# Norms behind message passing computed inside its last step, and front rows and columns stored in four parts

## What is computed

```
xn  = layernorm(x)
h_t = xn;  three times: h_t = GRU_t(segment_sum((h_t @ W_t)[src] * (type == t), dst), h_t)
g   = leaky(layernorm(xn + h_0 + h_1 + h_2) * gamma + beta)      # slope 0.1
x1  = x + g + attention(xn)
out = x1 + experts(layernorm(x1))                                 # top 2 of 8 experts
```

## Time and profile before

| | us |
|---|---|
| median of 3 runs (3695.35, 3696.33, 3705.32) | 3696.33 |
| the profiled execution, its own time | 3672.03 |
| its span, first to last instruction | 3670.3 |
| TensorE busy in it | 2890.1 (79%) |
| VectorE busy | 1716.4 (47%) |
| ScalarE busy | 804.0 (22%) |
| GpSimd busy | 1475.2 (40%) |

### The profile page before, as it was taken

The page is one execution under the profiler, slowest core; times in us unless marked ns, Lnnn a source line. Parts: engine busy times, 40 slices in busy tenths (PEclk is TensorE's granted clock), DMA queues, the critical chain, the costliest instruction groups (busy, mean ns, idle before and its releaser), DMA issues. The chain is left out here.

```text
span 3670.3 us, 50411 instructions
## 1 busy us (share of the span) xinstructions
PE 2890.1 (79%) x15593; PEld 1858.2 (51%) x15593; DVE 1716.4 (47%) x3495; ACT 804.0 (22%) x1522; POOL 1475.2 (40%) x1508
## 2 busy tenths in 40 slices
PE   1589688889488888977888889688888933899991
PEld 1344455555264444555444446454444533788881
DVE  4379677771155555534454554254555556100002
ACT  1321244442211111141111113111111111233320
POOL 0000144440466666326666660666666200111124
PEclk6689798885699999988999999799999965799995
DMA  1200000001444444333444442433333133022213
GB/s 42 79 1 1 1 0 0 0 2 31 151 126 135 120 131 129 115 112 114 134 129 131 135 132 71 144 113 116 114 116 115 46 80 116 24 83 82 81 47 95
DMA packets 172350, 311.49 MB, mean 85 GB/s; under 512 B 26928, under 2 KB 125199, under 8 KB 171922
## 3 DMA queue, kind: packets, MB, share of 16 engines
q0 software_dynamic: 62016, 168.51, 16.0%
q1 hardware_dynamic: 110162, 140.82, 11.9%
HBM read 241.74 MB, written 67.49 MB: 84 GB/s over the span
## 5 line engine op out<-in xcount | busy, mean ns | idle before, releaser
L1420 POOL DMA_INDIRECT g_ring<-h_rows,idx x780 | 771.7, 989 | 369.6 <-issue 207.1
L1148 PE MATMUL g_pagg<-g_onehot,g_ring 128*128 128x144 f16 x4704 | 430.1, 231 | 229.5 <-issue 227.4
L1148 PEld LDWEIGHTS g_pagg<-g_onehot,g_ring 128*128 128x128 f16 x4704 | 342.1, 100 | 499.8 <-issue 483.0
L1319 DVE TENSOR_TENSOR g_agg<-g_agg,g_pagg 128x288 f32 x585 | 264.6, 452 | 574.9 <-remote 332.8
L1420 POOL DMA_INDIRECT g_ring<-xn_rows,idx x390 | 383.4, 983 | 188.3 <-issue 102.5
L864 POOL TENSOR_TENSOR mq_Fl<-mq_F,mq_Fh 128x448 f16<-128x448 f32 x168 | 191.4, 1166 | 490.4 <-ACT mq_Fh L849 483.0
L1322 DVE SCALAR_TENSOR_TENSOR g_onehot<-iota_keys,shift,keys 128x288 f16<-128x288 f16 x585 | 298.7, 512 | 0.9 <-issue 0.6
L1225 PE MATMUL g_pr<-g_agg,g_wc 128*128 128x448 f32 (+1 forms) x576 | 234.3, 526 | 23.0 <-DVE g_agg L1319 12.9
L1268 ACT ACTIVATE g_nT<-g_t,g_bi 128x448 f32<-128x448 f32 (+1 forms) x144 | 89.5, 622 | 704.2 <-DVE g_t L1361 499.2
L1225 PE MATMUL g_pi<-g_agg,g_wc 128*128 128x448 f32 (+1 forms) x576 | 228.8, 517 | 7.0 <-issue 6.6
L1939 DVE TENSOR_TENSOR f_ys<-f_bank,f_b 128x256 f32<-128x256 f32 x58 | 24.6, 424 | 444.1 <-PE f_bank L1888 430.2
(11 more groups left out here) (337 smaller groups left out, 4211.5 us busy)
## 6 DMA issues: line engine op xcount, KB each, us to landing
f_w<-in_L_ffn_W SPq DMA_DIRECT2D x16, 1024.0 KB
h_cols<-g_hn SPq DMA_DIRECT2D x36, 448.0 KB
h_rows<-g_rows SPq DMA_DIRECT2D x36, 448.0 KB
g_hT<-h_cols SPq DMA_DIRECT2D x36, 448.0 KB
g_ring<-h_rows,idx POOLq DMA_INDIRECT x780
g_hT<-xn_cols SPq DMA_DIRECT2D x18, 448.0 KB
slots_out<-f_ys SPq DMA_DIRECT2D x58, 128.0 KB
g_ring<-xn_rows,idx POOLq DMA_INDIRECT x390
```

Source lines behind the costliest of these rows:

```text
L1148: mm = e.matmul(pg[:, k * TYPES:(k + 1) * TYPES, :].rearrange("p t d -> p (t d)"), ring[:, slab, c, o:o + P], hot[:, c, :], start=(c == 0 ...
L1319: e.tensor_tensor(agg[:, :, bass.ds(o, DT)], agg[:, :, bass.ds(o, DT)], pagg[b % BANKS][:, :, :], ALU.add).then_inc(S["added"], 1)
L1420: e.indirect_dma_start(ring[:, b % SLABS, c, :], None, tables[s], bass.IndirectOffsetOnAxis(ap=idx[:, o:o + 1], axis=0)).then_inc(landed[b ...
```

## The change

It has three parts.

1. `normalise` stores rows and columns in four parts of seven tiles, each as soon as its tiles are through (784 KB a part).
2. `gnn_out` and `dve_normalise` are gone, and with them `h_sums`. In the last step each half is normalised right from `ptr` on VectorE, in a fixed pattern. For a half that is turned in unit u (`ENDS`): SyncE loads its part of `acc_rows` (unit u); statistics of `ptr` and a Sqrt (u+1); `levels` = first norm (u+2), times gamma plus beta (u+2); leaky step and addition of the parked x + attention (u+3); statistics of the sum and a Sqrt (u+4); second norm, and SyncE stores the sum to `acc_rows` and the norm to `xf_rows` (u+5). ScalarE's copy of `ptr` falls away. A unit in which one half is at u+1 and the one before it at u+4 is called a visit below. The last step runs six iterations past its last unit.
3. `ffn` starts by loading `rows` from `xf_rows` in four parts, TensorE's gate stage waits for the part it needs, and `acc` is loaded from `acc_rows` behind the second expert's weights.

The diff, cut to its core:

```diff
@@ normalise, sync
-                    e.wait_ge(n_l, TILES)
-                    e.dma_start(rows.rearrange("(i p) c -> p i c", p=PT), gm[:, :, :]).then_inc(n_o, 16)
-                    e.wait_ge(n_c, TILES + 2)
-                    e.dma_start(cols, xnT[:, :, :]).then_inc(n_o, 16)
-                    e.wait_ge(n_o, 32)
+                    for i in range(0, TILES, 7):
+                        e.wait_ge(n_l, i + 7)
+                        e.dma_start(rows[i * PT:(i + 7) * PT, :].rearrange("(i p) c -> p i c", p=PT), gm[:, i:i + 7, :]).then_inc(n_o, 16)
+                        e.wait_ge(n_c, i + 7 + 2)
+                        e.dma_start(cols[:, :, i * PT:(i + 7) * PT], xnT[:, :, i * PT:(i + 7) * PT]).then_inc(n_o, 16)
+                    e.wait_ge(n_o, 16 * 8)
@@ gnn
+        ENDS = [(g, b, NU * (g + 1) + 3 * b) for g in range(NG) for b in range(halves(TYPES * NG * (STEPS - 1) + g))]
...
+        def visit(v):
+            return ([(o, 1) for o, (g, b, u) in enumerate(ENDS) if u + 4 == v] + [(o, 0) for o, (g, b, u) in enumerate(ENDS) if u + 1 == v])
...
+        def act_spreads(e, v):
+            for o, k in visit(v):
+                e.wait_ge(S["moments"], moments_at(o, k))
+                e.activation(spread[k][:, :], inverse[k][:, :], ACT.Sqrt).then_inc(S["spread"], 1)
+
+        def dve_moments(e, v, step):
+            for o, k in visit(v):
...
+                for c in range(2):
+                    step(e.bn_stats(stat[:, c, :], ptr[:, c, :] if k == 0 else z[:, c, :]))
+                for c in range(2):
+                    step(e.bn_aggr(mean[k][:, c, :], stat[:, c, :]))
+                e.tensor_scalar(inverse[k][:, :], mean[k][:, :, 1], 1e-5, None, ALU.add).then_inc(S["moments"], 1)
+
+        def dve_level(e, v, step):
+            for o, k in visit(v - 1):
...
+                e.wait_ge(S["spread"], moments_at(o, k))
+                step(e.reciprocal(inverse[k][:, :], spread[k][:, :]))
+                if k == 0 and o >= 2:
+                    e.wait_ge(out_store[o % 2], 32 * (o // 2))
+                for c in range(2):
+                    if k == 0:
+                        ins = e.tensor_scalar(z[:, c, :], ptr[:, c, :], mean[0][:, c, 0:1], inverse[0][:, c:c + 1], ALU.subtract, ALU.mult)
+                    else:
+                        ins = e.tensor_scalar(park[:, c, :], z[:, c, :], mean[1][:, c, 0:1], inverse[1][:, c:c + 1], ALU.subtract, ALU.mult)
+                ins.then_inc(S["levelled" if k == 0 else "final"], 1)
+
+        def dve_scale(e, v, step):
...
+                if u + 2 == v:
...
+                    step(e.tensor_tensor(z, z, scales[:, 0:1, :].to_broadcast([PT, 2, C]), ALU.mult))
+                    step(e.tensor_tensor(z, z, scales[:, 1:2, :].to_broadcast([PT, 2, C]), ALU.add))
+                if u + 3 == v:
+                    step(e.scalar_tensor_tensor(out=z, in0=z, scalar=0.1, in1=z, op0=ALU.mult, op1=ALU.max))
+                    e.wait_ge(parked_in[o % 2], 16 * (o // 2 + 1))
+                    e.tensor_tensor(z, z, parked[:, 2 * (o % 2):2 * (o % 2) + 2, :], ALU.add).then_inc(S["outer"], 1)
@@ gnn, sync, last step
+                for v in range(UNITS + 6):
...
+                    for o, (g, b, u) in enumerate(ENDS):
+                        a = node_at(g) + 2 * b * PT
+                        if u == v:
...
+                            e.dma_start(parked[:, 2 * (o % 2):2 * (o % 2) + 2, :], acc_rows[a:a + 2 * PT, :].rearrange("(a p) c -> p a c", p=PT)).then_inc(parked_in[o % 2], 16)
+                        if u + 5 == v:
+                            e.wait_ge(S["outer"], o + 1)
+                            e.dma_start(acc_rows[a:a + 2 * PT, :].rearrange("(a p) c -> p a c", p=PT), levels[:, 2 * (o % 2):2 * (o % 2) + 2, :]).then_inc(out_store[o % 2], 16)
+                            e.wait_ge(S["final"], o + 1)
+                            e.dma_start(xf[a:a + 2 * PT, :].rearrange("(a p) c -> p a c", p=PT), parked[:, 2 * (o % 2):2 * (o % 2) + 2, :]).then_inc(out_store[o % 2], 16)
@@ gnn, scalar and vector
                     for v in range(UNITS):
                         act_unit(e, s, v)
                         act_turn(e, s, v)
+                        if last(s):
+                            act_spreads(e, v)
...
-                        if v:
+                        if last(s):
+                            dve_level(e, v, step)
+                        elif v:
                             dve_lo(e, s, v - 1)
...
                             dve_candidate(e, s, v)
+                        if last(s):
+                            dve_scale(e, v, step)
+                            dve_moments(e, v, step)
@@ ffn, sync
+                for i in range(4):
+                    e.dma_start(rows[:, 7 * i:7 * i + 7, :], xf[7 * i * PT:(7 * i + 7) * PT, :].rearrange("(i p) c -> p i c", p=PT)).then_inc(rows_in[i], 16)
...
-                for i in range(0, TILES, 7):
-                    e.wait_ge(S["rows"], i + 7)
-                    e.dma_start(xf[i * PT:(i + 7) * PT, :].rearrange("(i p) c -> p i c", p=PT), rows[:, i:i + 7, :]).then_inc(S["kept"], 16)
                 load(1)
+                e.dma_start(acc[:, :, :], acc_rows.rearrange("(i p) c -> p i c", p=PT)).then_inc(S["acc_in"], 16)
@@ ffn, tensor
-                    e.wait_ge(S["rows"], i + 1)
+                    if i % 7 == 0:
+                        e.wait_ge(rows_in[i // 7], 16)
```

More of the change, by code:

```diff
@@ L1123, in turn_after @@
         def turn_after(s, v):
-            u = v - (NU if last(s) else 2)
+            if last(s):
+                return next(((g, 0, b) for o, (g, b, u) in enumerate(ENDS) if u == v), None)
+            u = v - 2
             if u < 0:
                 return None
-            g, t, b = (u // NU, 0, u % NU) if last(s) else (u // NU, u % NU // KC, u % KC)
+            g, t, b = u // NU, u % NU // KC, u % KC
             return (g, t, b) if b < halves(turn_number(s, g, t)) else None
@@ L1507, in _ @@
                     act_turn(e, s, UNITS)
+                    if last(s):
+                        for v in range(UNITS, UNITS + 6):
+                            act_spreads(e, v)
                     if not last(s):
@@ L1516, in _ @@
                 e.tensor_tensor(brz[:, :, :], bi[:, :, :], bh[:, :, :], ALU.add).then_inc(S["set"], 1)
+                step = counted(e, S["rank"], 0)
                 for s in range(STEPS):
@@ L1519, in _ @@
                     dve_batches(e, s, 0)
-                    for v in range(UNITS + 2):
+                    for v in range(UNITS + (6 if last(s) else 2)):
                         if v < UNITS:
@@ L1599, in ffn @@
-def ffn(nc, A, acc, ident, ones, xf, slots_out, out):
+                        if last(s):
+                            dve_scale(e, v, step)
+                            dve_moments(e, v, step)
+def ffn(nc, A, acc, acc_rows, ident, ones, xf, slots_out, out):
     with ExitStack() as ctx:
@@ L1647, in ffn @@
         px = bank[6][:, :].rearrange("p (k n) -> p k n", k=KC)
-        S = {n: sem(f"f_{n}") for n in ("stats", "dve", "var", "std", "rows", "turned", "copied", "logits", "set", "made", "gate_in", "zeroed", "kept",
+        S = {n: sem(f"f_{n}") for n in ("dve", "acc_in", "turned", "copied", "logits", "set", "made", "gate_in", "zeroed",
                                         "gap", "exp", "taken", "counts", "offsets", "ranks", "placed", "lane", "found", "idx", "bias",
@@ L1673, in pe_gate @@
             mm.then_inc(S["logits"], 1)
-        def dve_normalise(e, step):
-            with e.Fori(0, TILES) as i:
-                e.bn_stats(stats[:, bass.ds(i, 1), :].rearrange("p a c -> p (a c)"), acc[:, bass.ds(i, 1), :].rearrange("p a c -> p (a c)")).then_inc(S["stats"], 1)
-            e.wait_ge(S["stats"], TILES)
-            for i in range(TILES):
-                e.bn_aggr(mv[:, i, :], stats[:, i, :]).then_inc(S["stats"], 1)
-            e.wait_ge(S["stats"], 2 * TILES)
-            step(e.tensor_scalar(rstd[:, :], mv[:, :, 1], 1e-5, None, ALU.add))
-            e.sem_inc(S["var"], 1)
-            e.wait_ge(S["std"], 1)
-            step(e.reciprocal(rstd[:, :], std[:, :]))
-            for i in range(TILES):
-                e.tensor_scalar(rows[:, i, :], acc[:, i, :], mv[:, i, 0:1], rstd[:, i:i + 1], ALU.subtract, ALU.mult).then_inc(S["rows"], 1)
         def dve_choose(e, step):
```

176 lines of the change are left out of this document (77 added, 99 removed).

## The result

The changed kernel takes **3610.2 us** (median of 4 runs, 3606.8 to 3613.7), the kernel before on the same chip 3697.8 (4 runs, 3695.4 to 3705.3): a ratio of **0.976** (95% interval 0.9742 to 0.9778), 87.5 us less. The forecast was 3609.3, in a range of 3598 to 3636. The profiled execution of the changed kernel took 3606.8 us (span 3605.1), that of before 3672.0: only 65.2 us less, where the sum had forecast 87.0 and 3585.0. Those 22 us are the first thing to explain.

A forecast was written before the change was run, and what follows sets the result against it. TensorE was taken to pace the last step, GpSimd's gathers close behind, VectorE partly idle. Savings 75.0 + 14.0 - 2 = 87.0 us take the median from 3696.3 to 3609.3 us; range 3598 to 3636, 8 in 10.

The forecast's parts named there:

- I take the difference as constant: Profiled execution of the kernel before lies 24.3 us below the timed median; the same distance was assumed for the changed kernel.
- The stretch behind the step: From the last store to the gate stage, 100.9 us before: 75.0 us saved.
- the last sum: In the last group, VectorE without rest ends its last sum at 2973.9, not 2968.2.
- the tail: VectorE's remaining norm work from the last sum to the issue of the last store: 12.7 us.
- The load in parts: Gate stage's first seven tiles land in 5.2 us; rival, all 28 awaited: 15.4, giving 3619 to 3620, chance 0.05.
- The front: Ahead of `mix`, only the last quarter of rows and columns is left to land: 14.0 us saved (12 to 16.1).
- The cost inside the step: Last step's new norm work mostly hidden behind TensorE: +2 us, between 0 and +10.
- The one-hot row: TensorE's batches in groups 1 to 6 waited for VectorE's one-hot 4.8 us; over 10 us would show the prediction wrong.
- VectorE +113 us: Last step: 14 halves at 8.1 us each make VectorE busy 113 us more.
- New and old work of 7.8 us in 6.8: In a 448-column unit without batches, a visit's VectorE work exceeds the room, so `t1` comes about 1.2 us late.
- norms reach TensorE: Rival: each of 14 visits holds up a batch or bank 1.5 to 3.5 us; 3628 to 3656, say 3642; chance 0.17.
- Slower than before: Rival: VectorE's 113 us and the 29 table loads lie mostly on the path, at the batches: 3757; chance 0.03.

The follow-up runs named there:

- r_before: The kernel before, unchanged, profiled a second time, on the second kind of chip: 3402.5 us, ratio 1.0004.
- r_after: The changed kernel, unchanged, profiled and timed again on the second kind of chip: 3311.9 us, ratio 0.9729 to the kernel before.
- e_whole: Changed kernel with the last stage's rows loaded in one transfer of 28 tiles, not four of seven: 3616.6 us, ratio 0.978 to the kernel before.
- e_bare: Changed kernel without the norms of the first 10 of 14 halves, loads and stores kept: 3592.5 us, ratio 0.9713 to the kernel before, with other routes.
- e_front: Kernel before with only the first norm's rows and columns stored in four parts: 3389.7 us, ratio 0.9967 to the kernel before.
- r_after2: The changed kernel, unchanged, once more as reference on the second kind of chip: 3316.7 us, ratio 0.975 to the kernel before.
- e_pool: Changed kernel with gamma and beta of halves 12 and 13 done on GpSimd, not VectorE: 3318.4 us, ratio 0.9755 to the kernel before.
- e_four: Changed kernel with statistics and norms done four times in each half: 3741.5 us, ratio 1.0116 to the kernel before.
- e_twice: Changed kernel with statistics and norms done twice in each half: 3330.8 us, ratio 0.9797 to the kernel before.

## Why the prediction was right, and where it wasn't

- **The median** was met to 1 us, but with errors that partly cancel; that closeness is luck. The sum of the terms in the trace, 77.4 and 14.7 less what step 3 lost, is 82 to 90 with a loss of 2.4 to 9.6, and the interval of the measurement is 82 to 95.
- **"I take the difference as constant" failed.** The profiled execution was forecast at 3585.0 and took 3606.8. The 24.3 us between the profiled run of before and its median were no fixed distance, but one short execution, by the changed kernels' traces 14.6 us of it in steps 1 and 2. The changed kernel's profiled run lies among its timed ones. The safe anchor was the saving set against the median; that both gave the same number hid the mistake.
- **The stretch behind the step**: forecast 75.0, measured 77.4 and (r_before to r_after) 76.5. The last store was to be issued 16.9 us later than before; counted from TensorE's last unit it is 13.7 later (17.0 us behind it, before 3.3). Two terms were mis-sized: the last sum 3.2 us late, not 5.7, since VectorE still rested until 2955, and the tail 11.96 us, not 12.7. Against it, the last store to the next block took 3.9, not 3.74, and the first tile 5.9, not 5.3: by the chain it waits for `bg`, issued 0.9 behind the rows, a wait the prediction left out.
- **The load in parts** does come early, and is worth 9.1 us (e_whole). The rival in which it doesn't is excluded.
- **The front**: forecast 14.0, 14.7 in the trace, 11.8 (7 to 15) alone in the times.
- **The cost inside the step**: forecast +2, bounds 0 to 10. The instructions of ten of the 14 halves are 2.4 of it (e_bare), without the loads and stores. On the second kind of chip step 3 took 586.8 (mean of r_before and e_front) and 593.5 (r_after, r_after2, e_pool): 6.7 more, with 4 us of spread and over two chips; 4.1 of it lie ahead of unit 36 and 2.6 behind. That is within the bounds, but above the +2. 61 us more of VectorE add only 2.5 to that, so VectorE's sum isn't the cause; table loads, 14 loads and 28 stores in place of 8, and the later gates are left, and the runs don't part them. This is open.
- **The one-hot row was a weak witness.** The argument for free time and the sign of failure both rest on TensorE's waits for the one-hot, 4.8 us. On the second kind of chip the same kernel before has 51.1 us there (r_before, at the end of the last section), and e_four, held up by VectorE for up to 12.1 us at a time, only 4.2. So the row neither shows that VectorE is in time nor that it is late. What carries the argument is VectorE's idle time with e_twice and e_bare.
- **VectorE +113 us**: 107.6 measured.
- **Slips that didn't matter.** New and old work of 7.8 us in 6.8 makes `t1` 1.0 us late, not 1.2, and the range 3598 to 3636 is said to run to the rival's middle, which is 3642.
- **The rival "norms reach TensorE"** (21 to 49 us) is excluded for this kernel: step 3 lost 4 to 10 us in any pair of traces from one kind of chip, and e_twice and e_bare put only 2 to 3 us on the instructions. **"Slower than before"** can be reached. I had it slower once 89 us of the new work lie on the path, and e_four fits that with 131 (3741.5 less 0.976 x 3698.8). What the prediction lacked is how new work comes to lie there, which is not in proportion: +61 us of VectorE cost 14 us, +183 cost 131. The place, batches held up with gathers behind them, was right: in step 3 of e_four GpSimd waited 107.7 us for them (30.7 in the kernel before, 39.2 in the changed one).

## What to carry over

Work moved off the critical path into an engine's free time cost little here while a visit was shorter than the unit that covers it, and much once it was longer: compare burst with unit, not sum with sum. Where between 61 and 183 us more it turns, no run shows. What has no matrix work over it, the last visits and the tail, is paid in full; cost it apart. A wait that the profile doesn't name can still be another engine's: compare the timelines of both. Tie a forecast to the timed runs, and before using the distance between a profiled execution and them, compare stages that the change doesn't touch.

## What was not expected of the hardware

Both kernels differ by 8 to 9% between chips of the two kinds (3698 and 3401 us; 3610 and 3312 to 3317), and nearly all of it lies in message passing: 670 to 701 us a step (e_four's last step aside) against 586 to 608. `mix` and the gate stage are alike within about 1%, the stretch behind the step within 2%, and the experts 3% shorter. The gathers take the same there (985 and 990 ns each on GpSimd in step 1). Single matmuls of one batch stand apart on the first kind of chip, though the kernel has no wait between them. Timeline of TensorE, kernel before:

```profile
1335.68 0.23 PE L1148 MATMUL g_pagg<-g_onehot,g_ring 128*128 128x144 f16 x1 [0.79 <-issue]
1336.38 0.22 PE L1148 MATMUL g_pagg<-g_onehot,g_ring 128*128 128x144 f16 x1 [0.48 <-issue]
1337.10 0.35 PE L1148 MATMUL g_pagg<-g_onehot,g_ring 128*128 128x144 f16 x3 [0.49 <-issue]
```

What TensorE's matmuls of the batches waited for in the last step, kernel before, on the first kind of chip and on the second, and there what its weight loads waited for (total us, times, longest):

```profile
PE g_pagg L1148 <- issue: 65.5, 80, 3.3
```

```profile
PE g_pagg L1148 <- DMA g_ring<-h_rows,idx: 44.0, 53, 4.2
PEld g_pagg L1148 <- DVE g_onehot L1322: 51.1, 82, 2.8
```

On the second kind of chip the matmuls of the batches stood mostly for their gathers, and the weight loads, which can wait while TensorE still works, for the one-hot. On the first kind the profile hardly names either. Some of its "issue" can be such waits, as e_four shows, but the stops inside one batch can't. What these are is open. Absolute times of one chip say little about another's; the ratios to the kernel before (0.976 and 0.973 to 0.975) agree.
